# A recurrent mixing block and two feed-forward layers on one core: first chunk's mixing in full fp32, later weight splits

## The reference

```python
t   = rmsnorm(x, norm1_w)
xb  = causal_depthwise_conv(t @ Wx, conv_w, conv_b)        # 4 taps
r, i = sigmoid(xb @ Wa), sigmoid(xb @ Wi)
a   = exp(-8 * softplus(lam) * r)
b   = sqrt(max(1 - a*a, 1e-12)) * (i * xb)
h   = scan: h[s] = a[s] * h[s-1] + b[s]                    # along the sequence
h1  = x + (h * gelu(t @ Wy)) @ Wo
u   = rmsnorm(h1, norm2_w)
ffn = (gelu(u @ Wg) * (u @ Wu)) @ Wd                       # 256 -> 1024 -> 256
x1  = layernorm(x + h1 + ffn)
out = layernorm(x1 + relu(x1 @ W1 + b1) @ W2 + b2)         # 256 -> 1024 -> 256
```

## Time and profile before

| what | us |
|---|---|
| median of 3 runs (621.52 to 623.34) | 622.78 |
| the profiled execution | 621.15 |
| its span | 619.4 |
| TensorE busy | 601.3 |
| VectorE busy | 386.9 |
| ScalarE busy | 309.0 |
| GpSimd busy | 205.1 |

### The profile page before, as it was taken

How to read it: one execution, slowest core, us unless ns; L and a number is a source line. 1 busy time by engine, 2 the same in 40 slices (tenths; PEclk the granted TensorE clock), 3 DMA queues, 4 the chain that set the end, 5 groups by cost and what they waited for, 6 DMA issues and landing times.

```text
span 619.4 us, 9569 instructions
## 1 busy us (share of the span) xinstructions
PE 601.3 (97%) x3681; PEld 536.6 (87%) x3681; DVE 386.9 (62%) x698; ACT 309.0 (50%) x580; POOL 205.1 (33%) x307
## 2 busy tenths in 40 slices
PE   7999988999999999999999999999999999999996
PEld 6897877789988898889888898888988898888996
DVE  5795676736585747747477465748467473663565
ACT  4865733365453754447444644537544473322353
POOL 5614137211724135130732216241451405241131
PEclk9999999999999999999999999999999999999999
DMA  8601001000100001010010101001000100000011
GB/s 274 228 2 34 1 2 35 0 1 2 34 1 1 34 1 36 2 34 1 1 35 2 34 1 35 0 1 35 2 1 1 35 1 1 1 19 18 0 35 35
DMA packets 13085, 15.69 MB, mean 25 GB/s; under 512 B 600, under 2 KB 12272, under 8 KB 13040
## 3 DMA queue, kind: packets, MB, share of 16 engines
q1 hardware_dynamic: 13040, 15.09, 7.2%
HBM read 10.89 MB, written 4.19 MB: 24 GB/s over the span
## 4 chain that ended last, share of the span: by engine, by line
PE 86%; DVE 8%; ACT 2%; POOL 2%; issue 1%; DMA 1%; POOLq 0%; DVEq 0%
PE psum L313 17%; PE psum L315 17%; PE psum L314 17%; PE psum L321 10%; PE psum L323 10%; PE psum L322 10%; PE psum L328 3%; DVE xb L847 1%; POOL normed L1218 1%; DVE row L922 1%; DVE xv L883 1%; DMA xs<-in_L_attn_x_dram 1%; PE psum L445 1%; PE psum L443 1%; PE psum L441 1%
## 5 line engine op out<-in xcount | busy, mean ns | idle before, releaser
L1247 POOL TENSOR_SCALAR gu_hi<-gu_raw 128x512 fp32r<-128x512 f32 x64 | 50.8, 794 | 318.3 <-DVE gu_raw L945 318.3
L955 DVE TENSOR_TENSOR hid_lo<-hid_raw,hid_hi 128x512 fp32r<-128x512 f32 x56 | 45.5, 813 | 83.9 <-ACT hid_hi L703 83.9
L699 ACT ACTIVATE hid_raw<-psum,vecs 128x512 f32<-128x512 f32 x56 | 38.4, 686 | 114.0 <-PE psum L315 114.0
L945 DVE TENSOR_TENSOR gu_raw<-psum,gu_raw 128x512 f32<-128x512 f32 x64 | 44.1, 689 | 81.3 <-PE psum L315 78.9
L321 PE MATMUL psum<-w_d_hi,gu_hi 128*128 128x256 f32 x256 | 72.8, 285 | 2.4 <-DVE gu_lo L950 2.4
L321 PE MATMUL psum<-w_hi,hid_hi 128*128 128x256 f32 x256 | 71.7, 280 | 0.6 <-DVE hid_lo L960 0.4
L323 PE MATMUL psum<-w_hi,hid_lo 128*128 128x256 f32 x256 | 71.8, 281 | 0.0
L323 PE MATMUL psum<-w_d_hi,gu_lo 128*128 128x256 f32 x256 | 71.8, 280 | 0.0
L322 PE MATMUL psum<-w_lo,hid_hi 128*128 128x256 f32 x256 | 71.7, 280 | 0.0
L322 PE MATMUL psum<-w_d_lo,gu_hi 128*128 128x256 f32 x256 | 71.6, 280 | 0.0
L690 ACT ACTIVATE gu_raw<-psum 128x512 f32<-128x512 f32 x64 | 38.1, 596 | 49.1 <-PE psum L315 48.4
(11 more groups left out here) (166 smaller groups left out, 1574.4 us busy)
## 6 DMA issues: line engine op xcount, KB each, us to landing
xs<-in_L_attn_x_dram SPq DMA_DIRECT2D x8, 512.0 KB, 3.5
out_dram<-row SPq DMA_DIRECT2D x15, 256.0 KB, 2.2
raw<-in_L_ffn_W_dram SPq DMA_DIRECT2D x2, 1024.0 KB, 13.0
raw_gud<-in_L_attn_Wg_dram SPq DMA_DIRECT2D x1, 1024.0 KB, 8.4
raw_gud<-in_L_attn_Wu_dram SPq DMA_DIRECT2D x1, 1024.0 KB, 10.5
raw_gud<-in_L_attn_Wd_dram SPq DMA_DIRECT2D x1, 1024.0 KB, 12.7
raw_xyai<-in_L_attn_Wx_dram SPq DMA_DIRECT2D x1, 256.0 KB, 2.8
raw_xyai<-in_L_attn_Wy_dram SPq DMA_DIRECT2D x1, 256.0 KB, 3.0
```

Of the source, the lines that this page charges most:

```text
L699: nc.scalar.activation(hid_raw[:, w % SLOTS, :], bank[:, :], ACT.Relu, bias=vec("b1", m)).then_inc(relu_ready, 1)
L945: nc.vector.tensor_tensor(gu_raw[:, r % SLOTS, :], up_bank(r)[:, :], gu_raw[:, r % SLOTS, :], ALU.mult).then_inc(gu_ready, 1)
L955: nc.vector.tensor_tensor(hid_lo[:, w % SLOTS, :], hid_raw[:, w % SLOTS, :], hid_hi[:, w % SLOTS, :].bitcast(FP32), ALU.subtract).then_inc ...
L1247: nc.gpsimd.tensor_scalar(gu_hi[:, r % SLOTS, :], gu_raw[:, r % SLOTS, :], 1.0, 0.0, ALU.mult, ALU.add).then_inc(gu_hi_ready, 1)
```

## The change

It rewrites the lists of all five engines up to round 11.
- In the mixing of chunk 0, and in the x and y products of chunk 1, each product is one fp32 matmul on the unsplit weights and activations (`raw_step`, `raw_product`, `first_x`, `first_decay`, `first_out`). The splits of a, i, x, y and o move to rounds 0 to 4.
- x of chunk 0 is loaded in two halves, and squares, 1/rms, norm and transposes go by halves. The norm of chunk 0 moves from GpSimd to VectorE, that of u of chunks 0 and 1 to ScalarE (`first_norm_u`).
- y of chunk 0 comes after decay and input, and the decay and input products of chunk 1 move from ahead of round 0 into round 3. ScalarE does tanh, exponential, tanh, square and square root of chunk 1 in one block of round 3. The scans move to round 5, `mix_out(1)` goes behind down(5) in round 6, the splits of u of chunk 1 go by pairs, and down(7) goes ahead of gate_up(8).
- W1 and W2 are split in rounds 8 and 9; ScalarE waits in round 10 for lo of both before it writes x1T_hi. W1 is loaded after the splits of x, y, a and i, W2 after that of d: the raw copies share memory with other tiles. The squares of the first chunk's decay move from ScalarE to VectorE (`squared_decay`).
- Filler goes from 88 to 33 matmuls.

The core of the diff ("---" lines name the engine; the waits that only count semaphores anew are left out):

```diff
--- order of the loads (SyncE)
-    load_x(0)
+    for q in range(PAIRS):
+        load_first_x(q)
...
-    for n in ("x", "y", "a", "i"):
+    for n in ("x", "a", "i"):
         load_w(n)
     load_x(1)
-    for n in ("g", "u", "o", "d", "1"):
+    for n in ("y", "g", "u", "o", "d"):
         load_w(n)
     sync.dma_start(b2_rows[:, :], b2.partition_broadcast(P)).then_inc(b2_loaded, DMA)
+    sync.wait_ge(hi_split["d"], pieces["d"])
+    sync.wait_ge(lo_split["d"], pieces["d"])
     load_w("2")
...
+        if c == 2:
+            sync.wait_ge(wy_done, 2 * KD)
+            for n in ("x", "y", "a", "i"):
+                sync.wait_ge(hi_split[n], pieces[n])
+                sync.wait_ge(lo_split[n], pieces[n])
+            load_w("1")
--- TensorE: new functions
+    def transposed_by_pairs(src, c, ready, done, bank, fillers):
+        for q in range(PAIRS):
+            pe.wait_ge(ready, 4 * c + 2 * q + 2)
+            for tt in (2 * q, 2 * q + 1):
+                for f in range(KD):
+                    last = nc.tensor.transpose(pair_bank(bank, q)[:, f, (tt % 2) * P:(tt % 2 + 1) * P],
+                                               src[:, tt, f * P:(f + 1) * P], ident[:, :])
+            last.then_inc(done, 1)
+            keep_running(fillers[q], SECOND)
...
+    def raw_step(dst, n, m, k, moving):
+        return nc.tensor.matmul(dst, raw_weight(n)[:, k, m * P:(m + 1) * P], moving[:, k, :], start=(k == 0),
+                                stop=(k == KD - 1))
+    def raw_product(bank, n, moving, done):
+        for m in range(KD):
+            for k in range(KD):
+                last = raw_step(psum[bank + m][:, :], n, m, k, moving)
+            last.then_inc(done, 1)
...
+    def first_x(c):
+        pe.wait_ge(first_tT_ready, 4 + 2 * c)
+        raw_product(MIX, "x", first_tT[c], wx_done)
+    def first_decay(bank):
+        for k in range(KD):
+            pe.wait_ge(taps_added, taps_done(0, LOOKBACK - 1, k))
+            for m in range(KD):
+                last = raw_step(psum[bank + m][:, :], "a", m, k, xb)
+                if k == KD - 1:
+                    last.then_inc(wa_done, 1)
+    def first_out(bank):
+        for q in range(PAIRS):
+            for k in range(KD):
+                if q == 0:
+                    pe.wait_ge(hy_ready, k + 1)
+                for tt in (2 * q, 2 * q + 1):
+                    last = nc.tensor.matmul(half_bank(bank, tt), gy[:, k, toks(tt)], raw_weight("o")[:, k, :],
+                                            start=k == 0 and tt % 2 == 0, stop=k == KD - 1,
+                                            skip_group_check=True)
+            last.then_inc(wo_done, 1)
--- TensorE: rounds
         if r == 1:
-            pe.wait_ge(tanh_a_ready, 4)
+            pe.wait_ge(h1_ready, 2)
         elif r >= 2:
             pe.wait_ge(gelu_ready, r - 1 if r < KH else r)
+        if r == 0:
+            split_done("g")
         product(gate_bank(r)[:, :], "g", m, uT_hi, uT_lo).then_inc(gate_done, 1)
+        if r == 0:
+            split_done("u")
         if r >= 2:
...
-            pe.wait_ge(tanh_i_ready, 4)
+            pe.wait_ge(gy_ready, 2 * KD)
...
+        if r == KH:
+            down(r - 1)
         if units(r):
             gate_up(r)
+        if r == 3:
+            split_done("a", "i")
+            mix_decay(1)
+            mix_input(1)
...
         if r == 1:
             split_done("d")
-        if units(r - 1):
+        if units(r - 1) and r != KH:
             down(r - 1)
+        if r == 6:
+            split_done("o")
+            mix_out(1)
+        if r == 7:
+            transposed_by_pairs(normed, 1, u_ready, uT_done, MIX, (0, 0))
...
+        if r == KH:
+            split_done("x")
+        if r == KH + 4:
+            split_done("y")
         if r == LAG_UP:
-            split_done("1", "2")
+            split_done("1")
+        if r == LAG_DOWN:
+            split_done("2")
--- TensorE: prologue
-    nc.tensor.transpose(psum[GATE][:, 0:NV], vec_rows[:, :], ident[0:NV, 0:NV]).then_inc(vecs_transposed, 1)
-    keep_running(14, SECOND)
-    transpose_t(0)
-    keep_running(5, SECOND)
-    split_done("x")
-    mix_x(0)
-    split_done("y")
-    mix_y(0, bank=DOWN)
-    transpose_t(1)
-    keep_running(9, SECOND)
-    split_done("a", "i")
+    nc.tensor.transpose(psum[UP][:, 0:NV], vec_rows[:, :], ident[0:NV, 0:NV]).then_inc(vecs_transposed, 1)
+    keep_running(1, SECOND)
+    transposed_by_pairs(normed, 0, t_ready, tT_done, MIX, (2, 3))
+    pe.wait_ge(w_loaded["x"], DMA)
+    first_x(0)
+    keep_running(7, SECOND)
     pe.wait_ge(vecs_ready, 1)
-    mix_decay(0, bank=GATE)
-    mix_input(0, bank=SECOND)
-    mix_x(1)
+    pe.wait_ge(w_loaded["a"], DMA)
+    first_decay(GATE)
+    pe.wait_ge(w_loaded["i"], DMA)
+    raw_product(SECOND, "i", xb, wi_done)
+    pe.wait_ge(tap_done, 2)
+    pe.wait_ge(t_ready, 8)
+    transposed(normed, tT_done)
+    pe.wait_ge(w_loaded["y"], DMA)
+    raw_product(DOWN, "y", first_tT[0], wy_done)
+    first_x(1)
+    pe.wait_ge(tanh_a_ready, KD)
+    keep_running(4, GATE)
+    pe.wait_ge(w_loaded["o"], DMA)
+    pe.wait_ge(tanh_i_ready, KD)
+    first_out(SECOND)
     pe.wait_ge(gy_ready, KD)
-    mix_y(1, bank=DOWN)
-    pe.wait_ge(tanh_a_ready, KD)
-    keep_running(28, GATE)
-    split_done("o")
-    mix_out(0, bank=GATE)
-    pe.wait_ge(tanh_i_ready, KD)
-    keep_running(24, SECOND)
-    transpose_u(0)
-    mix_decay(1, bank=SECOND)
-    pe.wait_ge(gy_ready, 2 * KD)
-    mix_input(1, bank=DOWN)
-    split_done("g", "u")
+    raw_product(DOWN, "y", first_tT[1], wy_done)
+    transposed_by_pairs(normed, 0, u_ready, uT_done, GATE, (3, 5))
     for r in range(UNITS):
--- ScalarE: new functions, rounds, prologue
+    def first_norm_u(c):
+        if c == 0:
+            act.wait_ge(tT_done, 4)
+        else:
+            act.wait_ge(uT_done, 2)
+        for q in range(PAIRS):
+            act.wait_ge(rms2_rstd, 2 * c + q + 1)
+            for tt in (2 * q, 2 * q + 1):
+                nc.scalar.activation(normed[:, tt, :], h1[c][:, tt, :], ACT.Copy,
+                                     scale=rstd2[:, tt:tt + 1]).then_inc(u_ready, 1)
 
...
+        if r == LAG_UP:
+            act.wait_ge(lo_split["1"], pieces["1"])
+            act.wait_ge(lo_split["2"], pieces["2"])
...
         if mixing and p == 0:
             if m == 0:
+                weight_hi("a")
+                weight_hi("i")
+            if m == 1:
+                xb_hi(n)
+            if m == 2:
+                weight_hi("x", "n1")
+                weight_hi("y", "n1")
+            if m == 3:
+                tanh_decay(n)
                 exp_decay(n)
+                tanh_input(n)
                 square_decay(n)
-                act.preload_act_table(ACT.Gelu_apprx_tanh)
-            if m == 2:
                 gate_scale(n)
                 act.preload_act_table(ACT.Gelu_apprx_tanh)
-            if m == 1:
-                weight_hi("1")
-            if m == 3:
-                weight_hi("2")
             if m == 4:
+                weight_hi("o")
+            if m == 6:
                 hy_hi(n)
+                square_first_h1(n)
+            if m == 7:
+                first_norm_u(n)
+                split_hi_by_pairs(uT_hi, n, MIX, uT_done, uT_hi_ready)
...
+        if r == KH:
+            weight_hi("1")
+        if r == KH + 1:
+            weight_hi("2")
...
+    square_first_x()
+    act.wait_ge(vecs_transposed, 1)
+    nc.scalar.activation(vecs[:, :], psum[UP][:, 0:NV], ACT.Copy).then_inc(vecs_ready, 1)
     act.wait_ge(vecs_ready, 1)
...
-    weight_hi("x", "n1")
-    split_hi(tT_hi, tT_done, tT_hi_ready, 0)
-    square_x(1)
+    act.wait_ge(tT_done, 1)
+    for f in range(KD):
+        nc.scalar.activation(first_tT[0][:, f, half(0)], pair_bank(MIX, 0)[:, f, :], ACT.Copy,
+                             scale=vec("n1", f)).then_inc(first_tT_ready, 1)
     conv_start(0, 0)
     conv_start(0, 1)
-    gelu_y(0, bank=DOWN)
-    xb_hi(0)
-    split_hi(tT_hi, tT_done, tT_hi_ready, 1)
+    square_x(1)
+    weight_hi("g", "n2", ks=[0])
     tanh_decay(0, bank=GATE)
-    weight_hi("o")
     act.wait_ge(consts_ready, 1)
     exp_decay(0)
-    square_decay(0)
     tanh_input(0, bank=SECOND)
     gate_scale(0)
     act.preload_act_table(ACT.Gelu_apprx_tanh)
-    hy_hi(0)
+    gelu_y(0, bank=DOWN)
+    weight_hi("g", "n2", ks=[1])
+    weight_hi("u", "n2", ks=[0])
     conv_start(1, 0)
     conv_start(1, 1)
+    square_first_h1(0)
+    weight_hi("u", "n2", ks=[1])
+    first_norm_u(0)
+    split_hi_by_pairs(uT_hi, 0, GATE, uT_done, uT_hi_ready)
     gelu_y(1, bank=DOWN)
-    square_h1(0)
-    xb_hi(1)
-    split_hi(uT_hi, uT_done, uT_hi_ready, 0)
-    tanh_decay(1, bank=SECOND)
-    tanh_input(1, bank=DOWN)
     act.wait_ge(lo_split["g"], pieces["g"])
--- VectorE: new functions
+    def first_norm_t():
+        for q in range(PAIRS):
+            dve.wait_ge(rms1_rstd, q + 1)
+            for tt in (2 * q, 2 * q + 1):
```

(127 more changed lines are left out.)

170 lines of the change are left out of this document (102 added, 68 removed).

## The result

The change makes the kernel slower, by half a per cent. Its median is 625.86 us (20 runs, 623.97 to 627.13) against 622.75 us for the kernel before (20 runs, 621.52 to 624.51); the ratio is 1.0049, with a 95% interval of 1.0039 to 1.0058. The forecast was 622.2 with a range up to 625.5. The profiled execution of the changed kernel took 626.89 us and has a span of 625.1 us, 5.7 more than the span of before.

A forecast was written before the change was run, and what follows sets the result against it. TensorE, busy 97% of the span, was taken as the bound. mlp_up(0) 2.5 us earlier plus 1.9 for one clock fall gave -0.6: span 619.4 to 618.8, median 622.78 to 622.2 us, range 616.5 to 625.5.

The forecast's parts named there:

- Part 1: Prologue: first fp32 product at 8.4, fp32 products 0.88 us each, gate of round 0 at 42.2 against 56.49.
- the lower bound of 0.46: Prologue: an fp32 product of 512 columns as two single passes, 0.46 us, if a filler's record is bound by its weight load.
- The price of the splits of g and u: End of prologue, VectorE: one piece alone at 1.2 us, two beside GpSimd's splits at 4.2; uT_lo at 42.2.
- Part 3: Rounds 3 to 7: 37.4 us, with waits around the single table visit; gate_up(8) at 90.9, a lead of 8.1 us.
- Part 4: Rounds 8 to 10: uncovered W1 and W2 splits, 4.7 us; TensorE idles 5.3; mlp_up(0) 23.1 us after gate_up(8)'s start.
- Part 5: Clock at mlp_up(0): one fall behind the 5.3 us stall, costing 1.9 us, paid in full.
- The rival "slower": Rounds 8 and 9: W1 and W2 pieces take 2.1 us instead of 1.2 beside GpSimd; +3.6 us, 625.8; chance 0.20.
- other waits of 1.9 to 2.2 us do no harm: TensorE's waits: argument for the rival that the clock holds, with no fall, 620.3 us; chance 0.25.
- Part 2: Rounds 0 to 2: 11.1 us and 0.2 of wait, splits of a and i hidden; round 3 at 53.5.
- The anchor: Start of mlp_up(0), 116.52 before: the span moves by what it moves; forecast at 114.0, 2.5 us ahead.

The follow-up runs named there:

- experiment 1: The changed kernel with 22 fillers in the wait ahead of mlp_up(0) alone: 623.78 us, ratio 1.0027 to the kernel before.
- experiment 8: The kernel before with the splits of W1 and W2 moved to rounds 8 and 9, and what this needs: 628.24 us, ratio 1.0090.
- experiment 2: The changed kernel with filler at every wait of about 2 us and ahead of mlp_up(0): 622.30 us, ratio 1.0005 to the kernel before.
- the first four experiments: Experiment 1, experiment 2, experiment 3 and experiment 4, each an edit of the changed kernel; the kernel before, run beside them, had a median of 621.67 us.
- experiment 3: The changed kernel with add_x_h1(0), the sum x + h1 of chunk 0, moved from round 2 to round 3: 622.13 us, ratio 0.9995.
- experiment 9: The changed kernel with W2 split in round 3, W1 in rounds 5 to 7, W1 loaded earlier, add_x_h1(0) after W2's splits, filler in waits: 616.89 us.
- experiment 4: The changed kernel with W1 and W2 split in rounds 3 and 4 in place of 8 and 9: 619.65 us, ratio 0.9974.

## Why the prediction was wrong

**Right.** In the prologue (Part 1) the first fp32 product came at 9.14 for 8.4, and the records lie 0.44 apart, two to a product, which is 0.88 us as estimated from the filler's records; the lower bound of 0.46 is out. Round 0 started at 42.08 for 42.2, round 3 at 53.90 for 53.5. The price of the splits of g and u came out by luck: their three pieces ran at 1.25 us each and not at 2.1, but the second rstd came late, its GpSimd instruction taking 1.62 us, and with it the second half of uT. In Part 3 the waits were 1.82 for 1.9 ahead of down(4), 1.23 for 1.2 ahead of down(5) (experiment 1), 1.93 for 1.85 ahead of the o product. Part 4 held to a tenth: rounds 8 to 10 took 23.1 us (120.54 - 97.40) with a wait of 5.22 for 5.3, and the same 23.2 in the kernel before with only that edit (experiment 8). Part 5's price for a fall, 1.9 (2.0 by its own rows, 3.79 less 16 x 0.114), was near: 1.6 to 1.7. That the slow records at the start show what a fall costs was the author's estimate: the trace gives the stretch from 2 to 5 us a granted clock of 1.00. The rival "slower" gave 625.8 by splits at 2.1 a piece in rounds 8 and 9; VectorE's timeline has them at 1.2. Its number fits, its mechanism doesn't; that the sum `add_x_h1` slows a split beside it was right, but it happened in round 2.

**The step that failed: Part 5's count of clock falls.** Its sum has one fall of 1.9 us, in the stall of 5.3 us, and none in any other wait. No row of before shows what the clock does in a stall that long (the nearest is the end, 0.50 from 616.50 behind the last matmuls); the runs showed 0.50 behind 5.22 us in the changed kernel and behind 5.24 in experiment 8, so that one fall was right. For the shorter waits there was one reading, the 2.19 us ahead of 94.93 with the clock at 1.00, on which the rival's "other waits of 1.9 to 2.2 us do no harm" rests. One wait that did no harm was taken as the rule for all of its length. The waits which the prediction itself named ahead of down(4) and of the o product, and one that it missed, made the clock fall three more times; two of these cost time, the one behind down(4) was free. With filler in the waits and nothing else changed, `mlp_up(0)` comes 3.1 us earlier and the kernel gains 4.7 us of span, 2.7 by the ratios (experiment 2), where Part 5 had put all falls at 1.9.

The profile of before could not warn of it. It has a second wait of this length, and the clock stayed at 1.00 there as well:

```profile
81.31 0.38 PE L321 MATMUL psum<-w_d_hi,gu_hi 128*128 128x256 f32 x1 [1.84 <-DVE gu_lo L950]
```

But at 621.15 us it was one of the fastest executions. The 35 runs of the same kernel beside the first four experiments lie in three groups: 20 at 621.1 to 621.9 us with a mean granted clock of 0.997 to 1.000, 12 at 622.4 to 623.4 with 0.995 to 0.997, and 3 at 624.5 to 624.7 with 0.994 to 0.995. That reads as if the kernel before had falls too, in the executions that were not profiled, and as if the 1.63 us between its profiled execution and its median, which the sum of the prediction added as a constant, were one of them. None of the slower ones was profiled, so it is not shown.

**The second miss: Part 2's "a and i are split on ScalarE and VectorE in rounds 0 to 2, hidden by these products".** The subtractions were priced alone, and no queue was checked for what ran beside them. The change moves `add_x_h1(0)` into round 2 on GpSimd, and both engines slowed: the subtractions took 1.77 and 1.76 us for 0.68, the sum 2.98 for 2.54. The 4.19 us for two pieces in the earlier trace rows, beside 4.67 on GpSimd in the earlier trace rows, had been read and was used for the prologue alone. An estimate from the times alone: the sum's halves take 1.27 us each, the subtractions 0.6 behind one another, and 2 x 1.27 + 2 x 0.6 is 3.7 us if the four ran in turn; from 54.41 to the end of `w_a_lo` at 57.94 it took 3.5. That is within 0.2 us, but why the two engines slow each other was not shown. Removing the overlap is worth 3.4 us by the ratios, and 5.3 us at `gate_up(8)` in the profiled executions, with the fall behind it and the one ahead of `gate_up(8)` that went too (experiment 3).

**The sum again.** The anchor was forecast at 114.0. Of the 6.5 us to 120.54, the falls are 3.1 (two of the three), the wait for `w_i_lo` 2.0, round 3's later start 0.4; 1.0 is left open, part of it in the fillers of the kernel by which the falls were measured. With the sum out of the way and one fall, rounds 3 to 7 took 38.2 us (92.06 less 53.9) against 37.4. Behind the anchor the clock costs 1.7 for 1.9 (1.6 against experiment 2's kernel). The predicted span was 618.8, and 618.8 + 6.5 - 0.2 is the 625.1 measured. The medians differ by 3.1 us, less than the 5.7 of the spans, since the kernel before was profiled in one of its fastest executions and the changed one in one of its slowest.

**Why the change loses.** The fp32 products are dearer, 0.88 against 0.69 us each, but experiment 9 keeps them and wins; the new prologue with split products was not run. Nor is it mainly the table visit (0.9 us). The gain of the prologue is real: it stands in the kernel of experiment 9, 4.5 us ahead at the anchor. It is eaten by the splits of W1 and W2 in two rounds in which VectorE has no gap, by the sum beside the splits of a and i, and by clock falls behind three of the waits: for the splits, for `w_i_lo` beside the sum, and for `mT_lo` ahead of the o product.

**Open.** The length of a wait does not tell alone whether the clock falls. It fell behind waits of 1.82, 1.85, 1.93, 1.96, 2.00, 2.01 and 2.04 us, and behind all of 3 us and more (3.08 to 5.24). It did not fall behind 1.82 (down(4), experiment 1, and the wait ahead of 83.22, experiment 8), 1.84 and 2.19 (before) and 2.01 us (the decay product, experiment 4). Inside the rounds, waits up to 1.67 us never did it in the kernels profiled here. What decides among waits of the same length was not found.
